# The attention values: one three-pass product of 512 columns per slot instead of four fp32 products of 128

## What is computed

```python
x = x + 0.5 * ffn(layernorm(x))
n = layernorm(x)                                  # 8 sequences of 512 rows, 128 wide
q, k, v = n @ Wq, n @ Wk, n @ Wv                  # 16 heads of 64
attn = softmax(causal(q @ k.T / 8))               # per sequence and head
x = x + (n + concat_heads(attn @ v) @ Wo)
x = x + 0.5 * ffn(layernorm(x))
```

## Time and profile before

| | |
|---|---|
| median of 3 runs | 1597.46 us (1597.28 to 1597.79) |
| profiled execution | 1598.28 us, of which the span from first to last instruction is 1596.1 us |
| granted TensorE clock, mean | 0.995 of full speed |
| first feed-forward stage | from about 33 us (the first chunk's product) to about 435 us |
| attention | about 435 to 1194 us |
| second feed-forward stage | about 1194 us to the end |

### The profile page before, as it was taken

How to read it: one execution, slowest core, us unless ns; L and a number is a source line. 1 busy time by engine, 2 the same in 40 slices (tenths; PEclk the granted TensorE clock), 3 DMA queues, 4 the chain that set the end, 5 groups by cost and what they waited for, 6 DMA issues and landing times.

```text
span 1596.1 us, 29240 instructions
## 1 busy us (share of the span) xinstructions
PE 1543.7 (97%) x8704; PEld 1041.6 (65%) x8704; DVE 1157.9 (73%) x2733; ACT 777.1 (49%) x1855; POOL 330.9 (21%) x780
## 2 busy tenths in 40 slices
PE   2999999999989999999999999999989999999998
PEld 2666666666666666666666666666656666666665
DVE  6977787777767676776767676776668777877775
ACT  3344333342466656666666656666643443333422
POOL 2000000000144444444444444444320000000000
PEclk9999999999999999999999999999999999999999
DMA  6443333333200000000000000000003333333332
GB/s 188 134 153 102 113 102 104 114 108 114 67 1 2 1 1 1 0 0 0 0 0 0 0 0 0 0 0 1 1 20 115 116 105 117 114 112 117 105 121 86
DMA packets 58801, 97.15 MB, mean 61 GB/s; under 512 B 6144, under 2 KB 15360, under 8 KB 58752
## 3 DMA queue, kind: packets, MB, share of 16 engines
q1 hardware_dynamic: 58752, 96.53, 18.9%
HBM read 92.83 MB, written 3.67 MB: 60 GB/s over the span
## 4 chain that ended last, share of the span: by engine, by line
PE 47%; issue 29%; POOL 19%; DVE 3%; DMA 1%; POOLq 1%; ACT 0%; SPq 0%; DVEq 0%
PE banks L376 17%; POOL work L1272 16%; PE banks L200 9%; PE banks L202 9%; PE banks L201 9%; POOL pool_pace L1267 3%; PE banks L338 1%; PE banks L348 1%; DVE work L1061 1%; DVE work L1033 1%; POOLq L1266 0%; DMA bias<-in_gate_bias 0%; DVE bn L871 0%; DMA work<-cw_rows 0%; PE banks L519 0%
## 5 line engine op out<-in xcount | busy, mean ns | idle before, releaser
L693 ACT ACTIVATE work<-banks 128x512 f32<-128x512 f32 x336 | 200.7, 598 | 463.5 <-PE banks L202 444.1
L1033 DVE TENSOR_TENSOR work<-banks,work 128x512 f32<-128x512 f32 x336 | 231.7, 690 | 155.5 <-ACT work L693 150.6
L376 PE MATMUL banks<-work,wd 128*128 128x512 f32 x672 | 342.9, 593 | 0.3 <-DVE work L1061 0.3
L750 ACT ACTIVATE work<-banks,nmax 128x512 f32<-128x512 f32 (+3 forms) x512 | 263.9, 530 | 31.2 <-DVE nmax L1115 31.2
L1272 POOL TENSOR_SCALAR work<-work,rrec 128x512 f32<-128x512 f32 (+3 forms) x512 | 270.6, 542 | 1.6
L200 PE MATMUL banks<-xT_hi,wg_hi 128*128 (+1 forms) x336 | 248.3, 739 | 0.0
L1061 DVE TENSOR_TENSOR work<-work 128x512 f32<-128x512 f32 x320 | 224.3, 701 | 15.1 <-DVE work L1033 9.5
L1115 DVE TENSOR_REDUCE nmax<-banks 128x2 f32<-128x1024 f32 (+3 forms) x256 | 204.2, 819 | 15.1 <-PE banks L479 13.8
L1133 DVE COPY stage<-banks 128x512 f32<-128x512 f32 x256 | 175.3, 685 | 47.6 <-PE banks L490 47.5
L490 PE MATMUL banks<-small,work 128*128 128x128 f32 x1280 | 199.8, 279 | 7.0 <-POOL work L1272 6.0
L490 PEld LDWEIGHTS banks<-small,work 128*128 128x128 f32 x1280 | 147.8, 141 | 44.3 <-issue 17.3
(11 more groups left out here) (116 smaller groups left out, 2230.2 us busy)
## 6 DMA issues: line engine op xcount, KB each, us to landing
work<-cw_rows SPq DMA_DIRECT2D x320, 256.0 KB, 3.1
x<-in_x SPq DMA_DIRECT2D x8, 256.0 KB, 7.9
out_rows<-x SPq DMA_DIRECT2D x8, 256.0 KB, 2.4
cw_rows<-cwT SPq DMA_DIRECT2D x16, 96.0 KB, 1.9
stage<-in_w_gate SPq DMA_DIRECT2D x3, 448.0 KB, 5.7
stage<-in_w_up SPq DMA_DIRECT2D x3, 448.0 KB, 6.5
wd<-in_w_down SPq DMA_DIRECT2D x3, 448.0 KB, 8.3
small<-in_small SPq DMA_DIRECT2D x1, 576.0 KB, 4.2
```

The source lines that it names most:

```text
L376: pe.matmul(psY, wd[:, j * P:(j + 1) * P], z[part_slot(j)], start=j == 0, stop=j == HT - 1, skip_group_check=True).then_inc(s["down_ps"], 1)
L693: nc.scalar.activation(silu[j % 2], psG[j % 3], ACT.Silu) \
L750: m = nc.scalar.activation(prob[:, p % 2, i, o:o + w], ps[:, i, so:so + w], ACT.Exp, bias=nmax[:, p % 2, i, qb:qb + 1], accum_out=rsum[:, ...
L1033: tt(gated[j % 3], psU[j % 3], silu[j % 2], ALU.mult) \
```

## The change

The values of a slot are no longer those of one pair for all 512 rows, but those of four pairs (512 columns, eight heads) for one tile of 128 rows, k = 0 to 7 counting tile k mod 4 of half k div 4. They come from `mm3`: the high and low parts of the transposed rows are stationary, and 512 columns of the split `Wv` stream through. So `Wv` is loaded beside Wq and Wk and split with them (a third split on ACT and on POOL), and `wv` and `xT_whole` are gone, with one of the two copies of `a_xT_high`. A half is complete only after four slots, so values are made three slots ahead, and `a_prep` for the next sequence moves from slot 5 to slot 4 (DVE's `a_rows`, `a_residual` and `a_xT_low` one slot earlier too). [...] On ACT, `pT_copy` of part 3 moves behind the third part of the exponentials. The table of expert numbers in `small` loses its six-fold repetition (80 KB of 576).

```diff
-SMALL = 7 * P + E * TOPK + TB * G * G
+SMALL = 7 * P + E + TB * G * G
...
-        aw = [sb(f"aw_{n}", [P, 2, H * DK], F32R) for n in ("hi", "lo")]
+        aw = [sb(f"aw_{n}", [P, 3, H * DK], F32R) for n in ("hi", "lo")]
-        wv = sb("wv", [P, H * DK])
...
-            sp.dma_start(wv[:, :], wv_in).then_inc(s["attn_w_loaded"], 16)
+            sp.dma_start(attn_w[:, 2, :], wv_in).then_inc(s["attn_w_loaded"], 16)
...
-            def project_values(b, p):
-                for t in range(TB):
-                    m = pe.matmul(psC[:, t * P:(t + 1) * P], xT_whole[:, t * P:(t + 1) * P],
-                                  wv[:, p * P:(p + 1) * P], start=True, stop=True,
-                                  skip_group_check=True)
-                m.then_inc(s["v_ps"], 1)
+            def project_values(parity, k):
+                t, i = k % TB, k // TB
+                rows = slice(parity * CH + t * P, parity * CH + (t + 1) * P)
+                mm3(pe, psC, [x[:, rows] for x in xT_parts],
+                    [w[:, 2, i * CH:(i + 1) * CH] for w in aw], True, True).then_inc(s["v_ps"], 1)
...
-                if have_q:
+                if have_v:
                     wait_pT(1, n)
-                    project_values(b2, p2)
+                    if p == 5:
+                        pe.wait_ge(s["a_xT_lo"], b + 2)
+                    project_values((parity + (p >= 5)) % 2, (p + 3) % HP)
...
-                if p == 5 and not last:
-                    pe.wait_ge(s["v_sb"], n + 3)
+                if p == 4 and not last:
+                    pe.wait_ge(s["v_sb"], n + 4)
                     a_prep(b + 1, psC)
...
-                pe.wait_ge(s["v_sb"], 1)
-                project_values(0, 1)
+                for k in (1, 2):
+                    pe.wait_ge(s["v_sb"], k)
+                    project_values(0, k)
                 for p in range(HP):
-                    attn_slot(0, p, True, False)
-                with pe.Fori(1, NC - 1) as b:
-                    for p in range(HP):
-                        attn_slot(b, p, False, False)
+                    attn_slot(0, p, 0, True, False)
+                with pe.Fori(0, NC // 2 - 1) as i:
+                    for k in (1, 2):
+                        for p in range(HP):
+                            attn_slot(i * 2 + k, p, k % 2, False, False)
...
             def a_xT_high(b, ps):
                 act.wait_ge(s["a_xT_ps"], b + 1)
-                nc.scalar.activation(xT_whole[:, :], ps, ACT.Copy)
...
-                for part in PT_ACT:
-                    pT_copy(b, p, part, first and p < 2)
-                if p == 5 and not last:
+                if p == 4 and not last:
                     a_xT_high(b + 1, psC)
...
                 if have_s:
                     exp(*ahead(b, p, 1), 2, False)
+                for part in PT_ACT:
+                    pT_copy(b, p, part, first and p < 2)
...
-            for w in range(2):
+            for w in range(3):
                 pool.wait_ge(s["aw_hi"], w + 1)
                 nc.gpsimd.tensor_tensor(aw[1][:, w, :], attn_w[:, w, :], f32(aw[0][:, w, :]),
```

More of the change, by code:

```diff
@@ L115, in build @@
         prob = work[:, 0:4 * PW].rearrange("p (r i c) -> p r i c", r=2, i=2)
-        NV = 4
-        values = work[:, 10 * CH:].rearrange("p (k t d) -> p k t d", k=NV, t=TB)
+        values = [work[:, 10 * CH:].rearrange("p (t d) -> p t d", t=TB),
+                  sb("values", [P, TB, CH])[:, :, :]]
         x = sb("x", [P, NT, P])
@@ L506, in attend @@
                         o = i * PW + KB_OFF[kb]
-                        m = pe.matmul(psB[i * DK:(i + 1) * DK, kb * P:], values[:, p % NV, kb, i * DK:(i + 1) * DK],
+                        m = pe.matmul(psB[i * DK:(i + 1) * DK, kb * P:], values[p // TB][:, kb, p % TB * P + i * DK:p % TB * P + (i + 1) * DK],
                                       pT[:, p % 2, o:o + w], start=kb == 0, stop=kb == TB - 1,
@@ L524, in rows_out, with attn_slot @@
                 to_columns(psO, outT[:, :].rearrange("p (t d) -> p t d", t=TB)).then_inc(s["outT_ps"], 1)
-            def attn_slot(b, p, first, last):
+            def attn_slot(b, p, parity, first, last):
                 n = pair(b, p)
+                have_v = not (last and p >= 5)
                 have_s = not (last and p + 1 >= HP)
@@ L553, in attn_slot @@
                 if first and p == 0:
-                    pe.wait_ge(s["v_sb"], 2)
+                    pe.wait_ge(s["v_sb"], 3)
                 else:
@@ L597, in attn_slot @@
                     pe.wait_ge(s["sigmoid_done"], NC + 1)
-                elif have_q:
-                    pe.wait_ge(s["v_sb"], n + 3)
+                elif have_v:
+                    pe.wait_ge(s["v_sb"], n + 4)
                 else:
@@ L685, in ffn_chunk @@
                         row_std(3)
-                    if std_n == 3 and j >= AW_SLOT and j - AW_SLOT < 2:
+                    if std_n == 3 and j >= AW_SLOT and j - AW_SLOT < 3:
                         attn_split_hi(j - AW_SLOT)
@@ L729, in part_hi, with value_copy @@
                     .then_inc(s[("q_hi", "k_hi")[which]], 1)
[L731 to L736, removed]
+            def value_copy(b, k, first):
+                act.wait_ge(s["v_ps"], b * HP + k + 1)
+                if k % TB == 0 and not first:
+                    act.wait_ge(s["ctx_ps"], b * HP + k - TB)
+                nc.scalar.activation(values[k // TB][:, k % TB, :], psC, ACT.Copy) \
                     .then_inc(s["v_sb"], 1)
@@ L790, in attn_slot @@
                     exp(*ahead(b, p, 1), 1, False)
-                if have_q:
-                    value_copy(*ahead(b, p, 2), first and p < 2)
-                for part in PT_ACT:
-                    pT_copy(b, p, part, first and p < 2)
-                if p == 5 and not last:
+                if not (last and p >= 5):
+                    value_copy(*ahead(b, p, 3), first and p < 5)
+                if p == 4 and not last:
                     a_xT_high(b + 1, psC)
@@ L815, in attention @@
                 value_copy(0, 1, True)
+                value_copy(0, 2, True)
                 for p in range(HP):
@@ L1170, in attn_slot @@
                     rows_mean(b - 1, b - 1 + 2 * NC)
-                if p in (2, 3) and not last:
-                    a_rows(b + 1, False, (2 * (p - 2), 2 * (p - 2) + 1))
-                if p == 4 and not last:
+                if p in (1, 2) and not last:
+                    a_rows(b + 1, False, (2 * (p - 1), 2 * (p - 1) + 1))
+                if p == 3 and not last:
                     a_residual(b + 1)
```

23 lines of the change are left out of this document (11 added, 12 removed).

## The result

| | before | after |
|---|---|---|
| median of 6 runs | 1597.62 us (1597.28 to 1599.53) | 1607.14 us (1604.10 to 1609.20) |
| profiled execution | 1598.28 us, span 1596.1 | 1607.36 us, span 1605.2 |
| granted TensorE clock, mean | 0.995 | 0.990 |

The changed kernel is **slower**, by a ratio of 1.0056 (95% interval 1.0043 to 1.0069), some 9.5 us. The forecast was 1586.8 us, and the range ended at 1592. Both sign and size were wrong.

What follows compares the result with a forecast made beforehand. TensorE, busy 97% of the span, was taken as the bound; -12.6 + 0.5 + 0.45 - 0.4 + 1.4 = -10.65 us gave 1587.6 us profiled, 1586.8 us without the profiler. Forecast band 1583 to 1590, range 1580.5 to 1592.

Steps and rivals of the forecast that it cites:

- the product in the slots: Values product on TensorE: 0.80 us in place of 0.99, 61 in slots instead of 62, -12.6 us.
- the loop's two jumps: TensorE's loop of two sequences: each of two jumps back refetches its first packet, 0.7 us each, +1.4 us.
- copy of part 3, six middle sequences: ScalarE's copy behind the exponentials: q projection keeps room (0.9 us before, less 0.19), so no wait, 0.
- prologue: Before the first slot scores: a third product waits for the second value copy, +0.45 us (0 to +0.8).
- third split: Extra ScalarE copy and POOL subtraction delay VectorE and ScalarE: +0.5 us, bounds 0 and +1.9.
- start: Loading of the constants: 80 KB less lets the first work begin earlier, -0.4 us (0.6 at most).
- the count by columns: TensorE values product: passes cost by columns, eight short ones cheaper than three long; +13 us, 1610; chance 0.01.
- the lower bound: VectorE beside POOL's added subtraction: it catches up again, so the added split costs 0.
- first step: VectorE's rows and residual only change slots, with 27% of its time free: 0.
- rival 4: Copy of part 3 over 0.9 us late for the q projection; 0.4 us a slot, +24, 1622; chance 0.03.
- second step: TensorE's jumps back: a landing of 3.1 us less the queue's lead of 2.4, 0.7 us each.
- Rival 2: TensorE's jumps back stall in full, 3.1 us each: +4.8, 1591.6; with a second packet each 1598; chance 0.15.

Runs made afterwards that it cites:

- the one with both repairs: Changed kernel with ScalarE's copy of part 3 back before the third part of the exponentials and TensorE's six middle sequences written out: 1589.85 us, 0.9944.

## Why the prediction was wrong

The forecast was -10.65 us on the profiled execution; it came out 9.1 us longer. By the steps of the forecast:

| step | forecast | measured |
|---|---|---|
| the product in the slots | -12.6 | -0.20 us per slot, as forecast |
| the loop's two jumps | +1.4 | +9.9 |
| copy of part 3, six middle sequences | 0 | +5.8 (0.46 + 0.51 each) |
| the same in sequence 0 and the tail | 0 | about +1.2 and +1.6 |
| slots 0 and 1 | 0 | about +1.5 (no or little gain there) |
| prologue | +0.45 | +0.64 (q projection at 431.68 to scores at 446.21; before 431.77 to 445.66) |
| third split | +0.5 | 0 (q projection 0.1 us earlier, as is the start) |
| start | -0.4 | -0.1 (7.04, before 7.13) |
| behind the last slot | 0 | +1.5 (430.9 us, before 429.4) |

The differences from the forecast add up to about 20 us, and the miss is 9.1 + 10.65 = 19.75. The last row goes with the clock. From the start of the last slot's scores, 40 us in the kernel before, in after and in the kernel with the copy back (same columns as above):

```profile
1166.71:1206.71 40.00, 33.72 (x189) 21.29 (x189) 27.49 (x89) 15.25 (x39) 6.75 (x18) 0.91 0.16 55
1174.29:1214.29 40.00, 33.87 (x179) 21.11 (x179) 26.27 (x86) 14.71 (x37) 6.73 (x18) 0.87 0.15 44
1163.12:1203.12 40.00, 32.45 (x194) 20.59 (x194) 27.56 (x89) 15.71 (x41) 6.72 (x18) 1.00 0.17 56
```

Mean clocks of 0.91, 0.87 and 1.00 go with 429.4, 430.9 and 428.0 us to the end. Why the clock fell in one and not in another isn't shown.

**Right:** the price of the product, both shapes read off neighbours that match (0.99 and 0.80 us), and so the rejection of the count by columns. The trace of after has the pass of 512 columns at 0.23 us behind a first one of 0.34. Between the two written-out kernels, the one before and the one with both repairs, the profiled slots differ by 721.4 - 709.3 = 12.1 us in all, near the term of 12.6, though slot 1 gave nothing. (Their medians, 1598.66 and 1589.85, come from two chips and lie 8.8 apart.) The rule quoted in the prediction was quoted in half: "TensorE: Matmul & The Clock Gate" of the Trainium skill, section on the back-to-back issue gap, calls 134 and 518 cycles the spacing of isolated products, and gives 81 and 131 ns for a sustained stream. By these the eight short passes would cost more than the three long ones, which is the sign that was measured; the trace's 0.124 and 0.235 us are above both pairs. The third split did stretch a VectorE product to 2.06 us beside POOL's of 2.68 (416.07 to 418.75), and VectorE caught up, the lower bound. It didn't end with POOL's, as the prediction read for the first split, but 0.55 us behind it, as the first one had (410.79 and 410.25).

```profile
417.24 2.06 DVE L1062 TENSOR_TENSOR work<-work 128x512 f32<-128x512 f32 x1
```

**Failed, first step:** "VectorE's rows and residual only change slots, and it has 27% of its time free: 0", together with "nothing ahead of them gets later" in rival 4. The 0.9 us of room before the q projection was right for the slot that I read the earlier trace rows, one without row work. Slots 2 and 3 have row work ahead of the maximum. It puts the exponentials 1.85 us behind the value copy instead of 0.50, so 1.35 us later, which is more than the room. VectorE's free time is a mean; the row work stood on the chain maximum, exponentials, copy, projection, which the change had just closed. The rival's point, 0.9 us late, was the right one, and it is passed in two slots of eight. The kernel with the row work behind the maximum shows it: same order on ScalarE, no wait.

**Failed, second step:** "I take 3.1 - 2.4 = 0.7 each". The mechanism was as feared: the body of two sequences doesn't stay, packets come all through the loop, and the taken branch waits. The Trainium skill, "Runtime: NRT & Kernel Launch", section on instruction fetch mechanics, says that a taken branch stalls when its target isn't in the current window of two pages. The traces agree for the longer body, with 4.5 and 4.9 us; they don't agree on the window, for the old body of six packets jumped back five times in 0.21 us without being fetched again. The size was off in two ways. The branch less the lead of 2.4 us gives the idle time, as I had reckoned (4.5 to 4.9 less 2.4 is 2.1 to 2.5, near the 2.33 and 2.79 measured), but I had put one landing of 3.1 us where the branch took up to 4.9, with two packets ahead of PE's next work; and idle time was taken as the whole price, though the clock behind it fell to 0.56, which cost about as much again. Rival 2 put the jumps at 1.4 + 4.8 = 6.2 us, or 12.4 with a second packet each; the 9.9 measured lie between, and neither held the clock.

**Rivals:** 2 and 4 both happened. Rival 2 came out stronger than its +4.8 (+8.5), rival 4 weaker than its +24 (about 8.6). I had them as alternatives with 0.15 and 0.03 and no case for the two together, which is what made it slower: either alone left the kernel slightly faster than before (0.9990 and 0.9986). Of what was to show it, "a wait of the q projection for line 761" and the two gaps appeared, the latter 190 us apart, and with them 32 more instruction packets (59 against 27) instead of some 24.

Single runs of after lie between 1604.1 and 1609.2 us, with mean clocks of 0.992 to 0.989. I had put this spread down to the jumps; but the kernel without them spreads over 4.4 us, with 0.996 to 0.992, so the clock varies elsewhere too, as it does behind the last slot. A loop of one sequence, with the stationary rows in a fixed place instead of at two addresses, might keep the saving without longer code; it wasn't tried.

## What to carry to other kernels

Before moving an instruction on one engine, find the slot in which what feeds it is latest, not a typical one: where row work or a residual visits only some turns, the room has to be read there. A longer loop body can lose what the shorter one had: here a body of about six packets stayed on the core and one of about eleven didn't. See whether instruction packets stop while the old loop turns, and if they do, price each jump of a longer one with several packets and the clock behind the gap, or write the turns out. When two suspected costs are independent, the case in which both occur needs its own line among the rivals.

## What the runs showed of the hardware

- A loop whose code no longer stays on the core pays at every jump back: branches of 3.3 us (idle 1.35 us, one packet) and of 4.5 to 4.9 us (idle 2.3 to 2.8 us, two packets), against 0.21 us with the old body. A shift of the code changed 5.0 us of idle time in two jumps to 2.8 (one execution).
- Straight code is fetched without a stall: 53 to 55 packets with PE's sequences written out, and no gap. Unrolling cost nothing here, and rolling up did.
- Behind gaps of 1.1 to 1.7 us at four jumps the granted clock stayed at 1.00. Behind four of 2.3 to 2.8 us it didn't follow the length: behind 2.33 us it was 0.59 and 0.56 for 8 us, behind 2.79 us 0.71 and 0.86, behind 2.51 us 0.76 and 0.67, and behind 2.46 us 1.00.
- A VectorE product of two operands in SBUF, 0.70 us on average, took 2.56 and 2.06 us beside two of POOL's subtractions, of 2.4 and 2.7 us, and ended 0.55 us behind them.
